# A fused normalise and quantised two-layer block: more work to GpSimd, identity built on the chip, a new pixel pairing, new orders

## The chip, the cores and the metric

The kernel runs on one core of one Trainium2 chip. The time is that of one launch on the device, in microseconds. Before the change: 70.01 us, median of 3 runs (69.95 to 71.6).

## The reference, cut to what matters

`x` is 8 images of 24 channels of 64 x 64 pixels. For each pixel, with all sums over its 24 channels:

```python
def conv_ref(x):                       # a gate per pixel
    m = sobel_complexity(x)            # edges of the mean over channels, scaled to 0..1
    steps = adaptive_steps(m)          # step widths from m
    V = v0 + v1 + v2 + v3              # how many of four walks visit the pixel
    return x * (V / (V + 1e-06))[:, None]

def ffn_ref(x, W1, b1, W2, b2):        # 24 -> 96 -> 24
    h = relu(qlinear(x, W1, b1))       # qlinear: products of fp8 (e5m2) values,
    return qlinear(h, W2, b2)          # result and result + bias rounded to fp16

def _gn(v, G=32, eps=1e-05): ...       # (g - m) / sqrt(s + eps)
def _ln_c(v, eps=1e-06): ...           # mean and variance over the channels
...
```

In the kernel this becomes: the input is centred and divided by its deviation over the channels (`inv_std`); that, times the gate's share, is the first branch, which is added to the input; the sum is normalised again (`norm2`), rounded to fp8, sent through the two quantised layers, and the result is added. When the normalised image is even, up to rounding, its edges are all zero and the visits are known beforehand (`flat_share`). The kernel computes that case, tests it at the end (`flag`), and repeats the work with computed visits only if the test says so. In the runs here it doesn't.

## The kernel before, in words

**Layout.** 128 partitions hold 256 pixels each of 24 channels, cut in 8 groups (`NG`) of 32 pixels (`GPIX`). A group's tile is 128 x 24 x 32, 768 numbers a partition. Statistics are made in four units of 1, 1, 2 and 4 groups (`UNIT_SIZE`).

**Stages of a group.** The sum over the channels (group 0: a VectorE reduction; groups 1 to 3: TensorE passes with the identity, `sum_channels`; groups 4 to 7 together: 24 passes in four parts, `sum_late_channels`). `centre` subtracts the mean (VectorE), `square` squares (ScalarE), `sum_squares` adds over channels on TensorE, then `take_var`, a square root on ScalarE (`first_std`), a reciprocal (`inverse_std`), the gain and a second variance (`conv_gain`), a second root and reciprocal, and `second_norm`. Then two branches:

- `conv` multiplies the centred tile by the gain into `result`, on GpSimd for groups 0, 1, 4, 5, 6 and on VectorE for 2, 3, 7. GpSimd then issues a DMA that adds the pixels to `result` (`add_pixels`).
- `quantise` makes fp8 values, two bytes of which form one bf16 word. Four TensorE transposes (`turn`) bring 96 rows = 24 channels x 4 to the partitions. ScalarE copies them (`copy_turned`). `first_layer` makes three hidden tiles of 128 rows and 1024 columns, each rounded to fp16 by ScalarE (`round_hidden`), biased and clipped by VectorE (`bias_relu`), and turned to fp8 (`quantise_hidden`). `second_layer` is 24 matmuls, ScalarE rounds (`round_ffn`), VectorE adds the second bias (`second_bias`) into `ffn_out`. For groups 0 to 5 GpSimd issues a second accumulating DMA (`add_ffn_by_dma`); for 6 and 7 VectorE adds (`add_ffn`), group 7 in halves.

**What sets the order.** Each engine has one order written out by hand (`first_groups` in each block); instructions start in that order as their semaphores allow. SP's queue issues the eight loads of pixels, then the stores of groups 0 to 6, each behind its second accumulate. ScalarE's queue issues the constants in two transfers at the start and the store of group 7 at the end. GpSimd's order has, besides the waits for its operands, five others:

```python
pool.wait_ge(s.scaled_var, 2)      # before conv(s, 0)
pool.wait_ge(s.norm2, 2)           # before conv(s, 1)
pool.wait_ge(s.ffn_out, 1)         # before conv(s, 4)
pool.wait_ge(s.hidden_act, 8)      # before conv(s, 5)
pool.wait_ge(s.hidden_act, 11)     # before conv(s, 6)
```

`keep_busy` issues three matmuls on a tile of zeros. `cast_weights` turns weights and biases to fp8 on VectorE after the centring of group 0. `unevenness` and `flag` are the test.

## Time and profile before

| | us |
|---|---|
| median of 3 runs | 70.01 |
| lowest, highest | 69.95, 71.6 |
| span of the profiled execution | 69.4 |
| busy: TensorE, VectorE, ScalarE, GpSimd | 53.4, 54.9, 44.2, 24.1 |

The profiled execution's own time is not given apart from its span; the span runs from the first to the last instruction. The mean granted TensorE clock over it is 0.948 of full speed. The page also counts 1372 instructions and 12.51 MB moved by DMA. Busy time of an engine counts its work, not its waiting; DMA-issuing instructions are counted apart, with the time until their data landed.

### The profile page before, as it was taken

The numbers are of one execution on the slowest core, as the hardware profiler recorded it, in microseconds if no ns is written. First come the engines' busy times: TensorE is split into PE (matmuls) and PEld (weight loads), VectorE is DVE, ScalarE is ACT, GpSimd is POOL, SyncE is SP. The second block draws the span as 40 slices with busy tenths as digits, with TensorE's granted clock in tenths as the row PEclk, the third lists the DMA queues.
The fourth block names the chain that finished last, engine by engine and source line by source line (L and its number), as shares of the span: only waits on it lengthen the run. The fifth ranks groups of instructions, "written<-read, shape, count | busy, mean of one in ns | idle before, by whom it ended". The sixth has DMA issues, their size and how long they took to land.

```text
span 69.4 us, 1372 instructions
## 1 busy us (share of the span) xinstructions
PE 53.4 (77%) x486; PEld 37.7 (54%) x486; DVE 54.9 (79%) x120; ACT 44.2 (64%) x60; POOL 24.1 (35%) x25
## 2 busy tenths in 40 slices
PE   2993999999999999948859969899898989700000
PEld 1323999999999999817126427355532644600000
DVE  2059934989799999999999999999999999981000
...
GB/s 0 291 403 404 413 402 232 9 0 0 0 184 71 198 0 0 130 101 57 170 9 73 216 218 282 209 189 200 302 218 202 296 214 331 240 241 125 395 177 11
DMA packets 4619, 12.51 MB, mean 180 GB/s; under 512 B 512, under 2 KB 640, under 8 KB 4608
## 3 DMA queue, kind: packets, MB, share of 16 engines
q0 software_dynamic: 2016, 5.51, 39.6%
q1 hardware_dynamic: 2160, 5.90, 22.2%
...
HBM read 3.72 MB, written 3.15 MB: 99 GB/s over the span
## 4 chain that ended last, share of the span: by engine, by line
PE 28%; DVE 23%; issue 15%; ACT 15%; DMA 7%; SPq 1%; DVEq 0%; ACTq 0%
ACT hidden_rounded L426 10%; PE ps_ffn L546 8%; DMA pixels<-in_x 7%; PE ps_ffn L534 6%; PE ps_ffn L564 4%; PE ps_hidden L564 4%; DVE hidden_q L852 3%; PE ps_ffn L619 3%; DVE hidden_act L843 3%; DVE result L812 3%; ACT packed_t L417 2%; DVE packed L831 2%; ACT ffn_rounded L436 2%; DVE inv_std L788 2%; DVE inv_std L817 2%
## 5 line engine op out<-in xcount | busy, mean ns | idle before, releaser
L426 ACT ACTIVATE hidden_rounded<-ps_hidden 128x1024 f16<-128x1024 f32 x24 | 23.9, 1049 | 0.5 <-PE ps_hidden L597 0.5
L343 POOL TENSOR_TENSOR result<-centred,gain 128x768 f32<-128x768 f32 x5 | 9.4, 1887 | 17.3 <-DVE scaled_var L805 14.7
L597 PE MATMUL ps_hidden<-packed_t,w1q 96*128 96x512 fp8e5 x48 | 13.9, 380 | 1.7 <-ACT packed_t L417 1.2
L331 POOL DMA_DIRECT2D result<-pixels x8 | 9.1, 1131 | 9.1 <-DVE result L812 7.9
L843 DVE TENSOR_SCALAR hidden_act<-hidden_rounded,b1q 128x1024 f16<-128x1024 f16 x24 | 11.6, 487 | 0.1
L395 ACT ACTIVATE squares<-centred 128x768 f32<-128x768 f32 (+1 forms) x9 | 6.7, 764 | 5.2 <-DVE centred L774 5.2
L619 PEld LDWEIGHTS ps_ffn<-w2q,hidden_q 128*128 128x128 fp8e5 x168 | 7.5, 98 | 3.7 <-DVE hidden_q L852 2.0
L619 PE MATMUL ps_ffn<-w2q,hidden_q 128*128 128x96 fp8e5 x168 | 8.3, 206 | 1.3 <-DVE square_sums L781 1.2
L337 POOL DMA_DIRECT2D result<-ffn_out x6 | 6.5, 1082 | 7.6 <-DVE ffn_out L860 7.6
L564 PEld LDWEIGHTS ps_ffn<-squares,fixed 128*128 128x128 f32 x72 | 8.7, 191 | 0.6
L564 PE MATMUL ps_ffn<-squares,fixed 128*128 128x128 f32 x72 | 8.9, 276 | 0.0
L852 DVE TENSOR_SCALAR hidden_q<-hidden_act 128x2048 uint16<-128x2048 uint16 (+1 forms) x16 | 8.8, 551 | 0.1
L436 ACT ACTIVATE ffn_rounded<-ps_ffn 128x768 f16<-128x768 f32 x7 | 7.5, 1068 | 0.5 <-PE ps_ffn L619 0.4
L774 DVE SCALAR_TENSOR_TENSOR centred<-ps_values,pixels 128x768 f32<-128x768 f32 (+1 forms) x9 | 7.5, 856 | 0.1
L831 DVE TENSOR_TENSOR packed<-centred,ps_values 128x768 fp8e5<-128x768 f32 x8 | 7.4, 945 | 0.0
L417 ACT ACTIVATE packed_t<-ps_turned 96x512 bf16<-96x512 bf16 x8 | 4.9, 613 | 3.4 <-PE ps_turned L582 3.4
L597 PEld LDWEIGHTS ps_hidden<-packed_t,w1q 96*128 96x128 fp8e5 x48 | 3.6, 97 | 5.5 <-ACT hidden_rounded L426 2.0
L632 PE MATMUL ps_ffn<-warm 128*128 128x512 bf16 x18 | 4.9, 382 | 1.4 <-ACT ffn_rounded L436 1.4
L546 PE MATMUL ps_ffn<-pixels,fixed 128*128 128x128 f32 x48 | 5.7, 276 | 0.0
L546 PEld LDWEIGHTS ps_ffn<-pixels,fixed 128*128 128x128 f32 x48 | 5.5, 192 | 0.0
L534 PE MATMUL ps_ffn<-pixels,fixed 128*128 128x128 f32 x36 | 4.4, 277 | 1.1 <-DMA pixels<-in_x 1.1
L534 PEld LDWEIGHTS ps_ffn<-pixels,fixed 128*128 128x128 f32 x36 | 4.2, 192 | 1.6 <-issue 1.6
...
## 6 DMA issues: line engine op xcount, KB each, us to landing
pixels<-in_x SPq DMA_DIRECT2D x8, 384.0 KB, 6.5
result<-pixels POOLq DMA_DIRECT2D x8, 384.0 KB, 4.6
out<-result SPq DMA_DIRECT2D x7, 384.0 KB, 4.3
result<-ffn_out POOLq DMA_DIRECT2D x6, 384.0 KB, 5.4
...
out<-result ACTq DMA_DIRECT2D x1, 384.0 KB, 3.2
...
```

The costliest lines, as they stand in the source:

```text
L331: pool.dma_start(result[:, n], pixels[:, n], accum_op=ALU.add).then_inc(s.residual[n], 16)
L343: nc.gpsimd.tensor_tensor(result[:, n], centred[:, n], group_values(gain, n), ALU.mult).then_inc(s.conv_pool, 1)
L426: nc.scalar.activation(hidden_rounded[:, i % HIDDEN_BUFS], ps_hidden[:, i % 2], ACT.Copy).then_inc(s.hidden_rounded, 1)
L436: nc.scalar.activation(ffn_rounded[:, n % 2].rearrange("p (h j) m b -> p h b (j m)", h=2)[:, lo:hi], ffn_banks(n)[:, lo:hi, 0:JP * CQ].rea ...
L534: last = nc.tensor.matmul(ps_channel[u][:, n - UNIT_START[u]], ident, pixels[:, n, c:c + CB, :], start=(c == 0), stop=(c == C - CB))
L546: last = nc.tensor.matmul(ps_late_channels, ident, pixels[:, 4:NG, c, :], start=(c == 0), stop=(c == C - 1))
L564: last = nc.tensor.matmul(ps_square[u][:, n - UNIT_START[u]], ident, squares[:, n, c * GPIX:(c + CB) * GPIX], start=(c == 0), stop=(c == C ...
L597: last = nc.tensor.matmul(ps_hidden[:, i % 2, b * BANK:(b + 1) * BANK], w1q[:, t * P:(t + 1) * P], packed_t[:, n % 2].bitcast(E5M2)[:, b:: ...
L619: last = nc.tensor.matmul(ffn_banks(n)[:, half, at * CQ:(at + 1) * CQ], hidden_q[:, n % 2, t, col * P:(col + 1) * P].bitcast(E5M2)[:, 0::2 ...
L831: nc.vector.tensor_tensor(packed[:, n % 2].rearrange("p j (c q) b -> p j c (q b)", q=Q), centred[:, n].rearrange("p c (j k) -> p j c k", j ...
L843: nc.vector.tensor_scalar(hidden_act[:, n % 2, t], hidden_rounded[:, (n * TILES + t) % HIDDEN_BUFS], b1q[:, t:t + 1], 0.0, ALU.add, ALU.ma ...
L852: nc.vector.tensor_scalar(hidden_q[:, n % 2, lo:hi], hidden_act[:, n % 2, lo:hi].bitcast(U16), 1.0 / 256, None, ALU.mult).then_inc(s.hidde ...
```

## The change

1. The channel sums of groups 4 to 7 come from GpSimd: `fold_channels` adds the two halves of the channels, then halves again, for two groups at a time, and VectorE copies the sums. The TensorE passes (`sum_late_channels`) are dropped.
2. The identity (fp32 and bf16) is made on GpSimd by two selects over a tile of ones; it is no longer loaded or cast. The constants are one transfer on SP's queue, between the loads of pixels 3 and 4. GpSimd does the casts of weights and biases.
3. All eight products (`conv`) are GpSimd's, and the five other waits are dropped. The accumulate of the sums of group 0 stands behind product 6, that of group 1 behind product 7.
4. The rows of the hidden layer are ordered so that tiles 0 and 1 have the same bias per row: one `bias_relu` covers both, and `quantise_hidden` covers all three tiles (group 7: two and one). The rounded hidden tiles have room for two groups.
5. The two pixels that share a bf16 word are sixteen apart in their group, not neighbours; the 96 rows are ordered q, c. The second layer's columns then come out in plain order, so `round_ffn` is a plain copy, and `copy_turned` copies fp32 words. The host arranges pixels and weights to fit.
6. The fast pass of the test multiplies the channel sums by `inv_std` and compares with `PEAK_LIMIT`; `flag` stands last on VectorE.
7. The stores of groups 6 and 7 are both ScalarE's. The orders of all engines are new; those of VectorE and ScalarE are only named here: quantisers of later groups, folded sums and biases stand in other places, and `square(1)` follows the first roots.

```diff
-SUM_SETS = [(0, 1), (1, 2), (2, 4), (4, 8)]
+SUM_SETS = [(0, 1), (1, 2), (2, 4), (4, 6), (6, 8)]
+FOLDED = range(4, NG)
...
-FIXED = {"ident": P, "share": PIX, "w1": Q * HIDDEN, "w2": TILES * CQ, "b1": TILES, "b2": 2 * CQ}
+TWIN = 64
+FIXED = {"share": PIX, "w1": Q * HIDDEN, "w2": TILES * CQ, "b1": 2, "b2": CQ}
...
-CONV_ON_POOL = [0, 1, 4, 5, 6]
-CONV_ON_VECTOR = [n for n in range(NG) if n not in CONV_ON_POOL]
+PEAK_LIMIT = C * FLAT * 2.0 ** 22
 ADD_BY_DMA = range(0, 6)
...
+        def hidden_acts(n, t):
+            return 2 * n + (1 if t < 2 else 2)
...
-            for n in range(NG - 1):
+                if n == 3:
+                    sp.dma_start(fixed[:], fixed_in).then_inc(weights_in, 16)
+            for n in range(6):
                 store(flat_pass, n)
             uneven_map = is_uneven(sp)
...
+            def make_identity():
+                link(nc.gpsimd.memset(ones[:], 1.0))
+                for tile in (ident, ident_bf):
+                    nc.gpsimd.affine_select(tile[:], ones[:], [[-1, P]], ALU.is_equal, 0.0, base=0,
+                                            channel_multiplier=1).then_inc(ident_ready, 1)
+            def cast_first():
+                pool.wait_ge(weights_in, 16)
+                nc.gpsimd.tensor_copy(w1q[:], w1_in, saturate=False).then_inc(first_weights, 1)
+                link(nc.gpsimd.tensor_copy(b1e[:], b1_in, saturate=False))
+                nc.gpsimd.tensor_copy(b1q[:], b1e[:]).then_inc(first_bias, 1)
+            def cast_second():
...
+            def fold_channels(n):
+                pair = (n - FOLDED.start) // 2
+                half = folded[:, pair]
+                pool.wait_ge(pixels_in[n], 16)
+                pool.wait_ge(pixels_in[n + 1], 16)
+                link(nc.gpsimd.tensor_tensor(half, pixels[:, n:n + 2, 0:12, :], pixels[:, n:n + 2, 12:24, :], ALU.add))
+                link(nc.gpsimd.tensor_tensor(half[:, :, 0:6, :], half[:, :, 0:6, :], half[:, :, 6:12, :], ALU.add))
+                link(nc.gpsimd.tensor_tensor(half[:, :, 0:3, :], half[:, :, 0:3, :], half[:, :, 3:6, :], ALU.add))
+                link(nc.gpsimd.tensor_tensor(half[:, :, 0, :], half[:, :, 0, :], half[:, :, 1, :], ALU.add))
+                nc.gpsimd.tensor_tensor(groups_pixels(folded_sums, range(2 * pair, 2 * pair + 2)).rearrange("p (g s) -> p g s", g=2),
+                                        half[:, :, 0, :], half[:, :, 2, :], ALU.add).then_inc(folded_ready, 1)
...
             def add_pixels(s, n):
-                if n in CONV_ON_POOL:
-                    pool.wait_ge(s.conv_pool, CONV_ON_POOL.index(n) + 1)
-                else:
-                    pool.wait_ge(s.conv_vector, CONV_ON_VECTOR.index(n) + 1)
+                pool.wait_ge(s.conv, n + 1)
...
             def first_groups(s):
-                pool.wait_ge(s.scaled_var, 2)
+                cast_first()
+                fold_channels(4)
+                fold_channels(6)
+                cast_second()
                 conv(s, 0)
                 add_pixels(s, 0)
-                pool.wait_ge(s.norm2, 2)
                 conv(s, 1)
                 add_pixels(s, 1)
+                conv(s, 2)
                 add_pixels(s, 2)
+                conv(s, 3)
                 add_pixels(s, 3)
-                pool.wait_ge(s.ffn_out, 1)
                 conv(s, 4)
-                add_ffn_by_dma(s, 0)
                 add_pixels(s, 4)
-                pool.wait_ge(s.hidden_act, 8)
                 conv(s, 5)
                 add_pixels(s, 5)
+                conv(s, 6)
+                add_ffn_by_dma(s, 0)
+                add_pixels(s, 6)
+                conv(s, 7)
                 add_ffn_by_dma(s, 1)
-                pool.wait_ge(s.hidden_act, 11)
-                conv(s, 6)
-                add_pixels(s, 6)
+                add_pixels(s, 7)
                 add_ffn_by_dma(s, 2)
-                add_pixels(s, 7)
                 add_ffn_by_dma(s, 3)
                 add_ffn_by_dma(s, 4)
                 add_ffn_by_dma(s, 5)
             nc.gpsimd.memset(eps_c[:], EPS_LN_C).then_inc(eps_ready, 1)
             nc.gpsimd.memset(eps_t[:], EPS_LN_T).then_inc(eps_ready, 1)
+            make_identity()
...
-                nc.scalar.activation(packed_t[:, n % 2], turned_group(), ACT.Copy).then_inc(s.turned_copied, 1)
+                nc.scalar.activation(packed_t[:, n % 2].bitcast(F32), turned_words(), ACT.Copy).then_inc(s.turned_copied, 1)
...
-                i = n * TILES + t
-                act.wait_ge(s.first_layer, i + 1)
-                if i >= HIDDEN_BUFS:
-                    act.wait_ge(s.hidden_act, i - HIDDEN_BUFS + 1)
-                nc.scalar.activation(hidden_rounded[:, i % HIDDEN_BUFS], ps_hidden[:, i % 2],
+                act.wait_ge(s.first_layer, n * TILES + t + 1)
+                if n >= 2:
+                    act.wait_ge(s.hidden_act, hidden_acts(n - 2, t))
+                nc.scalar.activation(hidden_rounded[:, n % 2, t], ps_hidden[:, (n * TILES + t) % 2],
                                      ACT.Copy).then_inc(s.hidden_rounded, 1)
...
-                nc.scalar.activation(ffn_rounded[:, n % 2].rearrange("p (h j) m b -> p h b (j m)", h=2)[:, lo:hi],
-                                     ffn_banks(n)[:, lo:hi, 0:JP * CQ].rearrange("p h (b m) -> p h b m", b=2),
-                                     ACT.Copy).then_inc(s.ffn_rounded, 1)
+                nc.scalar.activation(ffn_rounded[:, n % 2].rearrange("p (h i) m -> p h (i m)", h=2)[:, lo:hi],
+                                     ffn_banks(n)[:, lo:hi, 0:JP * CQ], ACT.Copy).then_inc(s.ffn_rounded, 1)
...
-            act.dma_start(fixed[:, 0:FIXED_AT["share"]], fixed_in[:, 0:FIXED_AT["share"]]).then_inc(ident_in, 16)
-            act.dma_start(fixed[:, FIXED_AT["share"]:], fixed_in[:, FIXED_AT["share"]:]).then_inc(weights_in, 16)
...
-            wait_result(act, flat_pass, NG - 1)
-            act.dma_start(out[NG - 1], result[:, NG - 1]).then_inc(flat_pass.stored, 16)
+            for n in (6, 7):
+                wait_result(act, flat_pass, n)
+                act.dma_start(out[n], result[:, n]).then_inc(flat_pass.stored, 16)
...
-            def sum_late_channels(part):
-                if part == 0:
-                    for n in range(4, NG):
-                        pe.wait_ge(pixels_in[n], 16)
-                    pe.wait_ge(sums_taken, 1)
-                for c in range(part * 6, (part + 1) * 6):
-                    last = nc.tensor.matmul(ps_late_channels, ident, pixels[:, 4:NG, c, :],
-                                            start=(c == 0), stop=(c == C - 1))
-                if part == 3:
-                    last.then_inc(sums_ready, 1)
...
             def first_groups(s):
                 sum_channels(1)
+                sum_squares(0)
                 sum_channels(2)
-                sum_squares(0)
                 sum_channels(3)
                 sum_squares(1)
-                sum_late_channels(0)
-                sum_late_channels(1)
-                sum_late_channels(2)
-                pe.wait_ge(ident_cast, 1)
+                pe.wait_ge(ident_ready, 2)
                 turn(s, 0)
-                sum_late_channels(3)
                 pe.wait_ge(first_weights, 1)
                 pe.wait_ge(var_taken, 1)
                 first_layer(s, 0, 0)
...
+                if lo in FOLDED:
+                    dve.wait_ge(folded_ready, i - 2)
+                    nc.vector.tensor_copy(sums, groups_pixels(folded_sums, range(lo - FOLDED.start, hi - FOLDED.start))).then_inc(sums_taken, 1)
...
-                nc.vector.tensor_tensor(packed[:, n % 2].rearrange("p j (c q) b -> p j c (q b)", q=Q),
-                                        centred[:, n].rearrange("p c (j k) -> p j c k", j=JP),
-                                        group_values(norm2, n).rearrange("p c (j k) -> p j c k", j=JP),
+                nc.vector.tensor_tensor(packed[:, n % 2].rearrange("p j (q c b) -> p (j q) c b", q=Q, b=2),
+                                        centred[:, n].rearrange("p c (b i) -> p i c b", b=2),
+                                        group_values(norm2, n).rearrange("p c (b i) -> p i c b", b=2),
...
-            def bias_relu(s, n, t):
+            def bias_relu(s, n, lo, hi):
                 dve.wait_ge(first_bias, 1)
-                dve.wait_ge(s.hidden_rounded, n * TILES + t + 1)
+                dve.wait_ge(s.hidden_rounded, n * TILES + hi)
                 if n >= 2:
-                    dve.wait_ge(s.hidden_q, 2 * (n - 1))
-                nc.vector.tensor_scalar(hidden_act[:, n % 2, t], hidden_rounded[:, (n * TILES + t) % HIDDEN_BUFS],
-                                        b1q[:, t:t + 1], 0.0, ALU.add, ALU.max).then_inc(s.hidden_act, 1)
+                    dve.wait_ge(s.hidden_q, n - 1)
+                nc.vector.tensor_scalar(hidden_act[:, n % 2, lo:hi], hidden_rounded[:, n % 2, lo:hi],
+                                        b1q[:, lo // 2:lo // 2 + 1], 0.0, ALU.add, ALU.max).then_inc(s.hidden_act, 1)
...
-                nc.vector.tensor_tensor(ffn_out[:, n].rearrange("p c (j k) -> p j c k", j=JP)[:, lo:hi],
-                                        ffn_rounded[:, n % 2, lo:hi].rearrange("p j (c q) b -> p j c (q b)", q=Q),
-                                        b2q[:, None, :].broadcast_to([P, hi - lo, 2 * CQ]).rearrange("p j (c k) -> p j c k", k=K),
+                nc.vector.tensor_tensor(ffn_out[:, n].rearrange("p c (i q) -> p i c q", q=Q)[:, lo:hi],
+                                        ffn_rounded[:, n % 2, lo:hi].rearrange("p i (c q) -> p i c q", q=Q),
+                                        b2q[:, None, :].broadcast_to([P, hi - lo, CQ]).rearrange("p i (c q) -> p i c q", q=Q),
...
-            def unevenness():
-                xall = xg[:].rearrange("p h s -> p (h s)")
+            def scaled_sums():
                 dve.wait_ge(inv_std_ready, UNITS)
-                link(nc.vector.tensor_scalar(channel_mean[:], channel_sums, 1.0 / C, None, ALU.mult))
-                link(nc.vector.scalar_tensor_tensor(rest[:], channel_mean[:], -float(C), channel_sums, ALU.mult, ALU.add))
-                link(nc.vector.tensor_tensor(xall, rest[:], inv_std[:], ALU.mult))
-                nc.vector.tensor_reduce(quad[:, 0:1], xall, AX_X, ALU.max,
+                nc.vector.tensor_tensor(xg[:].rearrange("p h s -> p (h s)"), channel_sums, inv_std[:], ALU.mult).then_inc(scaled_sums_ready, 1)
+            def partition_peaks():
+                dve.wait_ge(scaled_sums_ready, 1)
+                nc.vector.tensor_reduce(quad[:, 0:1], xg[:].rearrange("p h s -> p (h s)"), AX_X, ALU.max,
                                         apply_absolute_value=True).then_inc(peak_ready, 1)
...
```

## Rows read from the trace of the kernel before

**Rows 1.** Stretches of 6 us: busy of each engine, granted clock, DMA share, GB/s.

```profile
42.00:48.00 6.00, 5.63 (x69) 3.52 (x67) 6.00 (x12) 6.00 (x9) 4.04 (x4) 1.00 1.01 211
48.00:54.00 6.00, 5.19 (x50) 2.34 (x48) 5.90 (x15) 6.00 (x9) 2.64 (x3) 1.00 1.00 236
```

**Rows 2.** Chain of waits in order of time: start, us, what.

```profile
13.26 4.02 PE ps_ffn L546 x36
...
17.50 1.39 PE ps_ffn L546 x12
...
62.24 0.56 DVE result L871
```

**Rows 3.** What SyncE's transfer queue waited for: us in total, times, longest.

```profile
SPq L308 <- DMA result<-ffn_out: 57.2, 6, 35.2
SPq L317 <- DMA out<-result: 3.3, 1, 3.3
```

**Rows 4.** Timeline of VectorE: start, us, instruction.

```profile
39.72 0.57 DVE L843 TENSOR_SCALAR hidden_act<-hidden_rounded,b1q 128x1024 f16<-128x1024 f16 x1
...
56.49 0.55 DVE L860 TENSOR_TENSOR ffn_out<-ffn_rounded,b2q 128x768 f16<-128x768 f16 x1
...
59.98 0.96 DVE L871 TENSOR_TENSOR result<-result,ffn_out 128x768 f32<-128x768 f32 x1
```

**Rows 5.** Timeline of GpSimd, products and accumulate issues.

```profile
15.57 1.82 POOL L343 TENSOR_TENSOR result<-centred,gain 128x768 f32<-128x768 f32 x1 [14.70 <-DVE scaled_var L805]
17.70 1.01 POOL L331 DMA_DIRECT2D result<-pixels  x1 [0.32 <-DVE centred L774]
18.45 2.12 POOL L343 TENSOR_TENSOR result<-centred,gain 128x768 f32<-128x768 f32 x1
...
38.16 1.85 POOL L343 TENSOR_TENSOR result<-centred,gain 128x768 f32<-128x768 f32 x1
40.30 1.19 POOL L331 DMA_DIRECT2D result<-pixels  x1 [0.30 <-POOL result L343]
...
57.58 1.06 POOL L337 DMA_DIRECT2D result<-ffn_out  x1 [1.62 <-DVE ffn_out L860]
```

**Rows 6.** Issue of the last accumulate (57.58 us); last number: us until landed.

```profile
result<-ffn_out POOLq DMA_DIRECT2D x1, 384.0 KB, 5.9
```

**Rows 7.** Stretches of 1 us, columns as in group 1.

```profile
11.00:12.00 1.00, 1.00 (x12) 1.00 (x11) 0.40 (x2) 0.26 (x1) 0.00 (x0) 1.00 0.42 160
62.00:63.00 1.00, 0.00 (x0) 0.00 (x0) 0.69 (x2) 0.00 (x0) 0.00 (x0) 0.61 0.14 35
63.00:64.00 1.00, 0.00 (x0) 0.00 (x0) 0.00 (x0) 0.00 (x0) 0.00 (x0) 0.50 0.35 134
```

**Rows 8.** Page, part 3: DMA queues with packets, MB, share of 16 engines.

```profile
q0 software_dynamic: 2016, 5.51, 39.6%
q1 hardware_dynamic: 2160, 5.90, 22.2%
```

**Rows 9.** Groups by line and shape: busy us, mean ns of one, idle before.

```profile
L843 DVE TENSOR_SCALAR hidden_act<-hidden_rounded,b1q 128x1024 f16<-128x1024 f16 x24 | 11.6, 487 | 0.1
...
L436 ACT ACTIVATE ffn_rounded<-ps_ffn 128x768 f16<-128x768 f32 x7 | 7.5, 1068 | 0.5 <-PE ps_ffn L619 0.4
L831 DVE TENSOR_TENSOR packed<-centred,ps_values 128x768 fp8e5<-128x768 f32 x8 | 7.4, 945 | 0.0
...
L395 ACT ACTIVATE squares<-centred 128x768 f32<-128x768 f32 x7 | 5.7, 836 | 1.9 <-DVE centred L774 1.9
...
L852 DVE TENSOR_SCALAR hidden_q<-hidden_act 128x2048 uint16<-128x2048 uint16 x8 | 5.5, 688 | 0.0
...
L417 ACT ACTIVATE packed_t<-ps_turned 96x512 bf16<-96x512 bf16 x8 | 4.9, 613 | 3.4 <-PE ps_turned L582 3.4
...
L754 DVE TENSOR_REDUCE ps_values<-pixels 128x32 f32<-128x768 f32 x1 | 1.5, 1455 | 0.0
...
L744 DVE CAST w1q<-fixed 96x384 fp8e5<-96x384 f32 x1 | 0.4, 356 | 0.0
```

327 lines of the change are left out of this document (153 added, 174 removed).

## The prediction

> **What bounds the kernel now.** I read the busy time by stretch first. From 42 to 54 us VectorE is busy 11.90 of 12 us and ScalarE all 12 [rows 1]: two engines fill that stage together, and the DMA engines' share is 1.01 and 1.00, so a third resource is full as well. The chain of waits shows what sets the start: TensorE's four parts of late channel sums (4.02 and 1.39 us, split by one transpose) stand on it [rows 2], and its last computed piece is the addition of group 7, over at 62.80. But the span is 69.4. What fills the rest is in the transfer queue's waits: SyncE waited 57.2 us in all for accumulating DMAs, and 3.3 us at the end for its last store [rows 3]. The sums of group 5 are ready at 57.04 [rows 4], their accumulate is issued at 57.58 [rows 5] and takes 5.9 us to land [rows 6], so at 63.5; only then can store 5 go, and store 6, whose data were added by 60.94 [rows 4], stands behind it on SP. Meanwhile the DMA engines do next to nothing from 62 to 64 (0.14 and 0.35) [rows 7].
>
> So there are two chains: compute, and GpSimd's issues with the DMA engines behind them. The queues say how heavy the second is [rows 8]: 39.6% of 69.4 us over 14 accumulates (8 of pixels, 6 of sums) is 1.96 us each with all 16 engines; 22.2% over 15 plain transfers is 1.03 each. Accumulates and stores together: 14 x 1.96 + 8 x 1.03 = 35.7 us.
>
> **What the change takes off the compute chain.** *TensorE:* 48 passes of late sums, 5.4 us [rows 2], go. *VectorE:* three products of the quantiser's size and form, 3 x 0.945 = 2.8; six casts of weights and one of the identity, the largest 0.356 [rows 9], about 1.7 together (bound 2.5). Twin tiles: 16 bias instructions of 1024 become 8 of 2048; the quantiser of the same kind takes 0.688 for 2048 and the bias 0.487 for 1024 [rows 9], so I take 0.75 for a twin, 8 x (0.974 - 0.75) = 1.8 (bounds 0 and 2.3). Merged quantisers: seven times two fixed parts become one, about 1.0. Two steps of the evenness test leave, a third of a quantiser's elements each, 0.8 (bounds 0.6 and 1.9). Together 8.1 us of 54.9 (the casts and part of the products lay beside other work). *ScalarE:* the copy of the transposes takes 256 words instead of 512 halves. 0.613 at 512 and 0.836 at 768 give 0.87 ns an element, so 0.39, 8 x 0.22 = 1.8. The rounding of the second layer no longer interleaves: 1.068 at 768 becomes 0.836, as the squares of the same size [rows 9]; 7 x 0.23 = 1.6. If word size or stride cost nothing, both are 0; bounds 0 and 3.4, and I take 3.4.
> The input: 3.57 MB instead of 3.72, and pixels 1 no longer share with the constants. At the before's 0.40 MB/us, over in the twelfth microsecond (share 0.42) [rows 7], pixels 1 land near 4.3, the constants at 7.3, pixels 5 at 9.3 (2.79 MB), pixels 7 at 11.2: on SP's queue the constants stand ahead of pixels 4 to 7 and hold them for 1.1. Centring groups 4 to 7 waits for the folds, not for these. The first layer's weights come with the constants and then GpSimd's cast, near 8.3; the first layer wants them after 12. The identity must be there by then: two selects after 0.9, bound 0.1 to 1.9 each (nothing, a product of six times the elements), covered by the 11 warm-up matmuls.
> Walking the new orders with these durations, the first transpose is copied near 12.7 instead of 17.5, the sums of group 5 are out near 52 instead of 57.0, and the last addition ends near 57.5: compute is some 5 us earlier.
>
> **One price against that.** The quantiser now reads `centred` in steps of 64 and 128 bytes, before in runs of 32 bytes. The one VectorE row that reads SBUF in 128-byte steps is the channel sum of group 0: 1.455 us for 768 elements, against 0.945 for the quantiser [rows 9]. Bounds per quantiser 0 and +0.51, for eight 0 and +4.1; I take +2 by halves, since that row is a reduction during the input, and both ends go into the range. It delays the additions, not GpSimd's chain, and costs 0 to 0.7 at the end. The sums of the second layer write runs of 8 bytes instead of 16; no row has such a step, 0 to +0.3 per instruction (half its 0.55), and the same cover.
> The Trainium skill ("SBUF — State Buffer", Door 1: The DMA port swizzle) says that lines are 16 bytes and that a stride with one access per line pays a penalty; by that rule every quantiser pays. The trace agrees as far as that one row goes.
>
> **The other chain.** GpSimd now casts, folds, forms all products and issues the same 14 accumulates. One product is 1.82 to 1.85 us (the one at 18.45 counts 2.12, but the issue in front of it ran until 18.71) [rows 5]. A fold of a pair of groups is 768, 384, 192, 64 and 64 elements; in proportion to the product 1.85 x 1568 / 768 = 3.8; no row shows a small GpSimd operation, and I take 0.1 on the whole for what each costs besides. Four self-waits lie in it: 0, or the 0.30 between product and issue [rows 5]; I take 0.1 each. Two folds: 8.6 (bounds 7.6 and 10.2). The second casts: no row for GpSimd, between VectorE's 0.8 and twice that; 1.2. Product 0 starts at 9.3 + 8.6 + 1.2 = 19.1, where it started at 15.57. Product to product with one issue is 2.88 early (15.57 to 18.45); in the busy stage 2.14 go by before the issue and the issue takes 1.19 instead of 1.01, 3.3 at most [rows 5]; at 2.9, product 6 starts at 36.5. Now the queue position matters: the accumulate of sums 0 stands behind product 6, at 38.4 (before 36.3), with pixels 6 behind it; that of sums 1 stands behind product 7, near 42.3.
> The DMA engines: pixels 0 to 5 are through by about 39. Left are two pixel and six sum accumulates and eight stores, 8 x 1.96 + 8 x 1.03 = 23.9. From 39.8 (issue plus 1.4) that is 63.7 if the engines never rest. They rested 1.5 us of two in the before while the last accumulate landed [rows 7]; store 5 waits for that again, +1.5. GpSimd's products now run with no wait that places them, so some start against VectorE's bias and quantiser instructions: I allow 1.2 (below). From the last byte to the end 2.3 us as now (about 67.1 to 69.4). Sum 63.7 + 1.5 + 1.2 + 2.3 = **68.7 us of span**. The before's span of 69.4 stands 0.6 under its median of 70.01, so I forecast 69.3. Moving store 6 to ScalarE's queue takes it from behind store 5, inside the 1.5. The test of evenness moves last on VectorE, near 58: at no cost, since the stores cover it by some 8 us; with that cover gone, under 1.
>
> **Rivals.**
> *A, the backlog swallows the gain* (my forecast): 68.6 to 71.4, chance 0.36. For it: the full DMA share from 42 us.
> *B, it comes through in part.* GpSimd is never held (-1.2), its folds are at the low bound (-0.8), stores 0 to 4 fill the hole (-1.0): 66.3 to 68.6, near 67. If the whole compute gain reached the end, 52 + (69.4 - 57.04) - 1.4 (store 6) + 0.6 is 63.6, which the 23.9 us of transfers forbid unless they start earlier. For it: VectorE and ScalarE both gain. Chance 0.35.
> *C, GpSimd and VectorE shut each other out, slower.* The before starts its products behind counts (scaled_var 2, norm2 2, ffn_out 1, hidden_act 8 and 11), and they fall on quantisers. Where one product's end met a bias (39.72, product over at 40.01), that took 0.57 instead of 0.487 [rows 4, 9], and was over 0.28 after the product's end [rows 5]: as if its stream had waited for the whole rest. The change drops these waits. A bias or quantiser that meets a fresh product is then held up to 1.85 - 0.2 = 1.65. With four such meetings VectorE loses 6.6, more than its 5 of gain, ffn_out 0 is late, and GpSimd, in order, holds pixels 6 and product 7 behind it. Everything from 39.8 on moves 3 to 4: 73. It decides from 2 us of delay of the first sum accumulate (40.5). Against it: no row shows a meeting longer than 0.3 us. Chance 0.29.
> The Trainium skill ("SBUF — State Buffer", Who interferes with whom) says that VectorE's two-port modes and GpSimd hold a shared port pair for a whole instruction, and the other is fully blocked. By that rule C is the outcome, 73; this trace agrees on 0.3 us of overlap only.
> *D, the new forms save ScalarE nothing* (word copy, plain rounding): additions 1.7 later, still under the transfers, 69.5; inside A.
>
> **Numbers.** 69.3. The range 66.4 to 73.3 holds B without its lowest tenth and C without its dearest part. Within 2% (68.6 to 71.4, about what a measurement of this kernel can tell from no change) 0.36, faster 0.35, slower 0.29.
>
> **What would show it.** Right: late passes gone from TensorE; the first product near 19; GpSimd without idle time until about 44; DMA share near 1 from 40 to the last accumulate; ffn_out 5 near 52 and the last addition near 57.5 with the end near 68.7. Wrong: bias instructions over 1 us beside products (C); quantisers at 0.95 or 1.45 settle the stride; the first store before 42 and idle DMA engines after 50 would mean B. If GpSimd's small folds cost over 0.5 each, the sum is 1.5 too low.

## The result and the profile after

The changed kernel takes 82.53 us, median of 4 runs (82.02 to 83.76); the kernel before, run on the same chip, 70.81 (69.95 to 71.61). The ratio is 1.175, 95% interval 1.165 to 1.185: slower by some 12 us, outside the range that was given (66.4 to 73.3), on the side of rival C. The ratio is taken over the executions within 1.5% of the fastest of each kernel, so it differs a little from the quotient of the two medians. The profiled execution has a span of 80.6 us.

**Busy time** of the changed kernel, from part 1 of its page:

```profile
PE 54.7 (68%) x438; PEld 36.3 (45%) x438; DVE 65.9 (82%) x94; ACT 41.9 (52%) x60; POOL 38.7 (48%) x47
```

VectorE should have lost 8.1 us and regained 2 for the new pairing (4.1 at most). It went up instead, from 54.9 to 65.9. Groups by line and shape of the changed kernel (busy us, mean ns of one, idle before) say where:

```profile
L843 DVE TENSOR_TENSOR packed<-centred,ps_values 128x768 fp8e5<-128x768 f32 x8 | 11.6, 1446 | 0.1
L864 DVE TENSOR_SCALAR hidden_q<-hidden_act 128x3072 uint16<-128x3072 uint16 x7 | 9.3, 1344 | 0.0
L855 DVE TENSOR_SCALAR hidden_act<-hidden_rounded,b1q 128x2048 f16<-128x2048 f16 x8 | 7.6, 945 | 0.2 <-issue 0.2
L855 DVE TENSOR_SCALAR hidden_act<-hidden_rounded,b1q 128x1024 f16<-128x1024 f16 x8 | 7.2, 905 | 0.6 <-ACT hidden_rounded L479 0.3 <-issue 0.3
...
L823 DVE SCALAR_TENSOR_TENSOR scaled_var<-gain,scaled_once 128x128 f32<-128x128 f32 x1 | 1.8, 1782 | 0.0
```

The quantiser is at 1446, not 945: the upper bound of the stride, to 0.01 us. The single bias went from 487 to 905 ns although nothing about it changed [rows 9]. That is no property of the instruction. The timeline of VectorE in the changed kernel (start, us, instruction), which answers to [rows 4], shows it spread over a few cases:

```profile
16.50 1.74 DVE L820 SCALAR_TENSOR_TENSOR scaled_once<-gain,square_sums 128x32 f32<-128x32 f32 x1
...
24.86 2.35 DVE L855 TENSOR_SCALAR hidden_act<-hidden_rounded,b1q 128x2048 f16<-128x2048 f16 x1
...
31.18 1.79 DVE L855 TENSOR_SCALAR hidden_act<-hidden_rounded,b1q 128x1024 f16<-128x1024 f16 x1
...
39.10 3.90 DVE L855 TENSOR_SCALAR hidden_act<-hidden_rounded,b1q 128x2048 f16<-128x2048 f16 x3
...
53.94 3.71 DVE L864 TENSOR_SCALAR hidden_q<-hidden_act 128x3072 uint16<-128x3072 uint16 x1
...
72.85 1.02 DVE L883 TENSOR_TENSOR result<-result,ffn_out 128x384 f32<-128x384 f32 x2
```

Beside it the timeline of GpSimd of the same kernel, which answers to [rows 5]:

```profile
16.38 1.81 POOL L373 TENSOR_TENSOR folded<-pixels 128x768 f32<-128x768 f32 x1
...
21.65 1.82 POOL L395 TENSOR_TENSOR result<-centred,gain 128x768 f32<-128x768 f32 x1
...
24.58 2.07 POOL L395 TENSOR_TENSOR result<-centred,gain 128x768 f32<-128x768 f32 x1
...
30.58 2.10 POOL L395 TENSOR_TENSOR result<-centred,gain 128x768 f32<-128x768 f32 x1
...
39.98 2.06 POOL L395 TENSOR_TENSOR result<-centred,gain 128x768 f32<-128x768 f32 x1
...
53.22 0.88 POOL L389 DMA_DIRECT2D result<-ffn_out  x1 [8.17 <-DVE ffn_out L872]
...
54.37 2.45 POOL L395 TENSOR_TENSOR result<-centred,gain 128x768 f32<-128x768 f32 x1
...
69.06 1.02 POOL L389 DMA_DIRECT2D result<-ffn_out  x1 [0.95 <-DVE ffn_out L872]
```

Read the two together. The twin bias of 24.86 starts 0.28 after a product that runs until 26.65, and ends at 27.21, 0.56 behind it. The bias of 31.18 starts inside the product of 30.58 (over at 32.68) and ends at 32.97. `scaled_once`, a step of 0.19 us elsewhere, starts 0.12 after the first fold addition of the second pair and takes 1.74. Where one step meets one product, it ends its own length, less some 0.2 at most, after GpSimd's instruction. There are eight such places; five are in the fences, the other three are `norm2` at 28.57 (1.20) and 43.89 (1.32) and `scaled_var` at 37.40 (1.78). With the lengths that each step has when alone, the lost time is 1.55 + 1.60 + 0.98 + 1.31 + 1.49 + 2.10 + 1.02 + 2.76 = 12.8 us, 1.55 of it from a fold, the rest from products. With the forecast's savings and the stride's upper bound that makes 54.9 - 8.1 + 4.0 + 12.8 = 63.6 against 65.9 seen. Most of the remaining 2.3 is in how steps are counted. Neighbouring steps of VectorE overlap a little in the trace: before, the durations of its 120 steps add up to 61.6 us for 54.9 of busy time, and in the changed kernel those of 94 steps to 70.6 for 65.9. The overlap shrinks by 1.9 us, so that the steps that go take less off the busy time than their durations say.

The stretches of the changed kernel fit this. Stretches of 6 us of the changed kernel (columns as in [rows 1]):

```profile
30.00:36.00 6.00, 2.73 (x18) 1.67 (x17) 6.00 (x6) 1.91 (x5) 3.55 (x3) 0.81 0.72 131
...
42.00:48.00 6.00, 1.28 (x7) 0.58 (x6) 5.93 (x7) 2.01 (x4) 2.75 (x3) 0.67 0.49 89
48.00:54.00 6.00, 6.00 (x37) 3.40 (x35) 6.00 (x10) 3.35 (x4) 0.78 (x2) 0.50 0.01 3
...
66.00:72.00 6.00, 5.32 (x81) 3.56 (x78) 4.61 (x9) 3.91 (x6) 1.88 (x2) 1.00 1.07 312
```

Where [rows 1] had a DMA share of 1.01 and 1.00, there is now 0.49 and 0.01, and TensorE works 1.28 us of six: VectorE alone is full. The waits of the changed kernel (us in total, times, longest) name the two that starve:

```profile
POOL result L389 <- DVE ffn_out L872: 15.4, 5, 8.2
PE ps_turned L616 <- DVE packed L843: 7.5, 3, 4.2
```

TensorE waited 4.2 us for a quantiser until 46.73, and after such pauses its granted clock stood at 0.50, the lower of its two levels (48 to 54). The SyncE queue waited longer for the accumulates than in [rows 3]:

```profile
SPq L320 <- DMA result<-ffn_out: 66.6, 6, 50.7
```

The last addition is over at 73.87 (62.80 before), the span 6.7 later (6.6 before). The tail is unchanged; compute is 11 us later.

### The profile page after: what moved, and what is told of

Read it like the earlier page. It is cut to its first block, busy times and chain, and to the rows that moved or that the text cites. A ratio compares the mean times of both kernels' runs of the same rounds, so it can differ in the third digit from the quotient of the medians.

```text
span 80.6 us, 1256 instructions
## 1 busy us (share of the span) xinstructions
PE 54.7 (68%) x438; PEld 36.3 (45%) x438; DVE 65.9 (82%) x94; ACT 41.9 (52%) x60; POOL 38.7 (48%) x47
## 3 DMA queue, kind: packets, MB, share of 16 engines
q1 hardware_dynamic: 2160, 5.97, 20.0%
## 4 chain that ended last, share of the span: by engine, by line
DVE 41%; PE 32%; ACT 10%; issue 8%; ACTq 0%; DVEq 0%
DVE hidden_act L855 10%; PE ps_ffn L651 8%; PE ps_hidden L631 7%; DVE packed L843 7%; DVE centred L792 7%; PE ps_ffn L749 6%; PE ps_ffn L664 5%; ACT hidden_rounded L479 5%; DVE ps_values L834 4%; ACT ffn_rounded L489 3%; DVE scaled_once L820 3%; DVE inv_std L829 2%; PE ps_turned L616 2%; PE ps_ffn L584 2%; ACT packed_t L471 2%
## 5 line engine op out<-in xcount | busy, mean ns | idle before, releaser
L395 POOL TENSOR_TENSOR result<-centred,gain 128x768 f32<-128x768 f32 x8 | 16.4, 2053 | 3.3 <-DVE gain L818 3.3
L855 DVE TENSOR_SCALAR hidden_act<-hidden_rounded,b1q 128x2048 f16<-128x2048 f16 (+1 forms) x16 | 14.4, 925 | 0.9 <-issue 0.5
L389 POOL DMA_DIRECT2D result<-ffn_out x6 | 6.4, 1072 | 15.4 <-DVE ffn_out L872 15.4
L598 PE MATMUL ps_ffn<-squares,ident 128*128 128x128 f32 x72 | 9.2, 280 | 3.8 <-ACT squares L449 3.8
L843 DVE TENSOR_TENSOR packed<-centred,ps_values 128x768 fp8e5<-128x768 f32 x8 | 11.6, 1446 | 0.1
L598 PEld LDWEIGHTS ps_ffn<-squares,ident 128*128 128x128 f32 x72 | 8.4, 191 | 5.4 <-issue 5.4
L864 DVE TENSOR_SCALAR hidden_q<-hidden_act 128x3072 uint16<-128x3072 uint16 (+2 forms) x9 | 10.4, 1172 | 0.0
L616 PE MATMUL ps_turned<-ident_bf,packed 128*96 128x128 bf16 x32 | 4.0, 259 | 7.5 <-DVE packed L843 7.5
L616 PEld LDWEIGHTS ps_turned<-ident_bf,packed 128*96 128x96 bf16 x32 | 3.0, 147 | 9.9 <-DVE packed L843 9.3
L664 PE MATMUL ps_ffn<-warm 128*128 128x512 bf16 x18 | 5.6, 423 | 0.6 <-ACT ffn_rounded L489 0.5
L749 PE MATMUL ps_ffn<-warm 128*128 128x512 bf16 x11 | 4.9, 632 | 1.3 <-DVE warm L1143 1.3
L872 DVE TENSOR_TENSOR ffn_out<-ffn_rounded,b2q 128x768 f16<-128x768 f16 (+1 forms) x9 | 4.4, 508 | 0.7 <-ACT ffn_rounded L489 0.7
```

Source lines behind the costliest of these rows:

```text
L395: nc.gpsimd.tensor_tensor(result[:, n], centred[:, n], group_values(gain, n), ALU.mult).then_inc(s.conv, 1)
L598: last = nc.tensor.matmul(ps_square[u][:, n - UNIT_START[u]], ident[:], squares[:, n, c * GPIX:(c + CB) * GPIX], start=(c == 0), stop=(c = ...
L616: last = nc.tensor.transpose(turned_group()[:, j * P:(j + 1) * P], packed[:, n % 2, j].bitcast(BF16), ident_bf[:])
L664: nc.tensor.matmul(ps_ffn[:, i % 2] if n < NG - 1 else ps_turned[:], warm[:, 0:P], warm[:], start=True, stop=True)
L749: nc.tensor.matmul(ps_ffn[:, i % 2], warm[:, 0:P], warm[:], start=True, stop=True)
L843: nc.vector.tensor_tensor(packed[:, n % 2].rearrange("p j (q c b) -> p (j q) c b", q=Q, b=2), centred[:, n].rearrange("p c (b i) -> p i c ...
```

## The experiments

Each is the changed kernel or the kernel before with the edit that is shown. The kernel before ran beside each, at 70.8 to 71.3 us in the median; where intervals are given they are of the ratio to it.

**Meetings by themselves.** A kernel of its own starts one product of the real size and then one VectorE step, 0.3 us later.

```python
nc.vector.tensor_copy(scr[:, 0:32], vals[:, 0:32]).then_inc(go, 1)   # the product starts
link(nc.vector.tensor_reduce(scr[:, 32:64], ..., AX_X, ALU.add))     # PSUM alone, 0.42 us
link(f())                                                            # the step to be met
```

> This kernel computes nothing of the reference; it measures single VectorE instructions of the case, first alone, then each issued about 0.5 us after GpSimd has begun a product of 128x768. Theory (GpSimd and VectorE shut each other out): the bias of 2048, the merged quantiser of 3072 and the two-input step of 128 end only after the product, so they take up to 1.5 us more than alone (bias 0.75, quantiser 0.95, two-input step 0.29), whatever their own size; the fp8 quantisers, which read one operand from PSUM, and the reciprocal take the same as alone. Three merged quantisers issued just before a product delay it or are delayed by it once. Rival (both only slow each other down in proportion): the two-input step of 0.29 gains under 0.2, the bias under 0.4. Stride: the quantiser that reads steps of 64 and 128 bytes takes 1.45, the one with runs of 32 bytes 0.95; the one that reads runs of 64 bytes and writes in steps of 48 bytes tells whether writing costs the same (1.45) or nothing (0.95).

VectorE's timeline in that kernel, then GpSimd's:

```profile
12.57 1.54 DVE L70 TENSOR_SCALAR ha<-hr,b 128x2048 f16<-128x2048 f16 x2 [4.27 <-DMA px<-in_x]
...
29.68 2.06 DVE L70 TENSOR_SCALAR ha<-hr,b 128x2048 f16<-128x2048 f16 x1
...
35.27 1.66 DVE L72 SCALAR_TENSOR_TENSOR s<-s 128x128 f32<-128x128 f32 x1
...
37.54 0.95 DVE L75 TENSOR_TENSOR pkn<-px,vals 128x768 fp8e5<-128x768 f32 x1
...
43.87 0.95 DVE L71 TENSOR_SCALAR hq<-ha 128x3072 uint16<-128x3072 uint16 x1
```

```profile
29.39 1.80 POOL L53 TENSOR_TENSOR prod<-px,gain 128x768 f32<-128x768 f32 x1 [28.95 <-DVE scr L90]
...
44.04 2.44 POOL L53 TENSOR_TENSOR prod<-px,gain 128x768 f32<-128x768 f32 x1 [0.61 <-DVE scr L100]
```

The bias of two tiles takes 0.77 alone (two in 1.54) and 2.06 when met; the small step 0.31 alone and 1.66 met; the quantiser 0.95 both times. Started first, the quantisation of hidden values keeps its 0.95, and the product behind it needs 2.44 for 1.80; of three in a row the first goes, the product follows, and the other two wait: 4.42 us in all instead of some 2.9. So each engine shuts the other out for the rest of its instruction, for some forms and not for others. The strided read costs 1.45 against 0.95, alone too.

**The kernel before without its five placing waits.** Only `pool.wait_ge(...)` lines are taken out:

```diff
-                pool.wait_ge(s.scaled_var, 2)
-                pool.wait_ge(s.norm2, 2)
-                pool.wait_ge(s.ffn_out, 1)
-                pool.wait_ge(s.hidden_act, 8)
-                pool.wait_ge(s.hidden_act, 11)
```

> The kernel before with the five waits dropped that place products 0, 1, 4, 5 and 6, and nothing else. Lock theory: three or four products start against two-input steps and biases, each holds VectorE up to 1.65 us, VectorE loses about 5 to 8 us and ends that much later: 74 to 77 us. Rival (the backlog of transfers decides): products and their accumulates start earlier, nothing else changes: 69 to 70.5 us.

It took 79.76 us, ratio 1.130 (1.119 to 1.142): 9 us, more than the 74 to 77 that I expected. All five products met a step (at 13.33, 17.38, 38.09, 41.99 and 50.05), 9.0 us in all. VectorE's row and GpSimd's of one of them:

```profile
41.99 2.80 DVE L838 TENSOR_SCALAR hidden_act<-hidden_rounded,b1q 128x1024 f16<-128x1024 f16 x1
```

```profile
42.04 2.46 POOL L343 TENSOR_TENSOR result<-centred,gain 128x768 f32<-128x768 f32 x1
```

The bias stands 0.05 us *ahead* of the product by the trace and is held all the same, and the product takes 2.46 instead of 1.8. An accumulate issue of GpSimd is still open there (41.48 to 42.67), but an issue need not hold anything: in the kernel without product work below, a merged quantisation that starts inside one (44.70, the issue from 44.56 to 45.78) takes its usual 0.96, so I put the held time down to the product. Three quarters of the whole loss are had without any other part of the change.

**The change with its pixels paired as neighbours again.** The second layer's rounding interleaves again with it, as before the change; nothing else is touched. The quantiser's lines, the changed kernel's with a minus:

```diff
-packed[:, n % 2].rearrange("p j (q c b) -> p (j q) c b", q=Q, b=2), centred[:, n].rearrange("p c (b i) -> p i c b", b=2)
+packed[:, n % 2].rearrange("p j (c q) b -> p j c (q b)", q=Q), centred[:, n].rearrange("p c (j k) -> p j c k", j=JP)
```

> The changed kernel with the pixel pairing of before (neighbours share a word, rounding of the second layer interleaves again); all else as changed. If VectorE bounds the changed kernel: eight quantisers save 0.50 each, 4.0 us, less up to 1.7 for the dearer rounding on ScalarE: 78 to 80 us against 82.5. If the transfers bound it, the stride was hidden: 82 to 83.

It took 81.54 us, ratio 1.158 (1.148 to 1.167). The quantiser was back at 946 ns and 4.0 us of work gone, but only 1.0 of them reached the end, where I expected 78 to 80 us: single biases now averaged 1156 ns against 905, as the steps slid to other products.

**Products 2, 3 and 7 back on VectorE**, in the changed kernel, with no placing waits:

```diff
+CONV_ON_POOL = [0, 1, 4, 5, 6]
-                    conv(s, n)
+                    if n in CONV_ON_POOL:
+                        conv(s, n)
+                conv(s, 2)      # VectorE, behind quantise(s, 2); 3 and 7 alike
```

> The changed kernel with products 2, 3 and 7 on VectorE again, behind the quantisers of the same groups; GpSimd's placing waits stay dropped. Lock theory: VectorE works 2.8 us more but is held by three products fewer, each worth up to 1.65 to 3: 79 to 82.5. Rival (GpSimd's backlog decides): GpSimd is free 6 us earlier, 78 to 80. If neither: VectorE's 2.8 is added, 85.

84.77 us, ratio 1.191 (1.175 to 1.207), where I expected 79 to 82.5: a miss, and an instructive one. VectorE's row shows three biases in a row (1.83 us of work) held by two products in a row:

```profile
39.66 6.58 DVE L866 TENSOR_SCALAR hidden_act<-hidden_rounded,b1q 128x2048 f16<-128x2048 f16 x3
```

How many products GpSimd forms is not what counts; where each falls is.

**The change without the work of the products.** Each product is cut to one channel, the rest of the tile is loaded while the transfers idle:

```diff
-nc.gpsimd.tensor_tensor(result[:, n], centred[:, n], group_values(gain, n), ALU.mult)
+nc.gpsimd.tensor_tensor(result[:, n, 0:1], centred[:, n, 0:1], group_values(gain, n)[:, 0:1], ALU.mult)
+                sp.dma_start(result[:, n], x[n]).then_inc(filled[n], 16)
```

> The changed kernel, but each GpSimd product works on 1 channel of 24, and the rest of its tile is filled by eight extra loads of x while the transfers idle (12 to 20 us); the product of 23 channels is left out. Theory (VectorE steps are held by products): of some 13 us of held time about 1.5 to 2 belong to the folds, so 11 go; the last addition comes at 63 to 66 instead of 73.9 and the time is 71 to 75 us. Rival (the new orders, the folds or TensorE's half clock cost the time): 79 us or more, with the bias steps at 0.75 and the span hardly shorter.

72.22 us (72.02 to 72.28): 10.3 less than the changed kernel. All orders, the stride, the folds, the input order and the filler matmuls are still there. VectorE's busy time is 54.9 (11.0 less), the single bias is at 485 ns, and TensorE and its clock are back by themselves:

```profile
42.00:48.00 6.00, 5.17 (x64) 3.25 (x63) 5.20 (x9) 4.44 (x7) 3.04 (x5) 1.00 0.46 97
```

One meeting is left, that of `scaled_once` with a fold (1.73 at 15.88). The 10.3 us hold GpSimd's own time for the products too, but GpSimd had time to spare (15.4 us of waiting for sums above). The half clock was a consequence: no fill was added here, and TensorE's mean granted clock went from 0.858 to 0.941.

**The change with its late channel sums back on TensorE** and no folds:

```diff
-                fold_channels(4)
-                fold_channels(6)
+                sum_late_channels(0)       # TensorE; parts 1 and 2 follow,
+                sum_late_channels(3)       # part 3 behind turn(s, 0)
```

> The changed kernel with the late channel sums back on TensorE as before and no folds. Theory: the folds hold only 1 or 2 small steps (about 1.5 us) and their removal lets the products start 8 us earlier, onto other steps that they can hold, and TensorE gets 5.4 us back: 80 to 84 us, no clear gain. Rival (the folds' 8.6 us on GpSimd and the late additions behind them are the cost): 77 us or less.

84.97 us (83.84 to 86.0): no gain, as expected, though 1 us above the range. Product 0 now starts at 10.66, 11 us earlier, and with it the meetings (`scaled_var` of 32 values 0.99 in the mean, `norm2` 0.86).

**The useful parts on the kernel before.** Twin tiles with one bias, merged quantisation of hidden values, the shorter test of evenness, store 6 on ScalarE; all placing waits stay.

```diff
-                bias_relu(s, n, 0)
-                bias_relu(s, n, 1)
+                bias_relu(s, n, 0, 2)
-                quantise_hidden(s, n, 0, 2)
-                quantise_hidden(s, n, 2, 3)
+                quantise_hidden(s, n, 0, 3)
```

> The kernel before with only twin tiles and one bias for two, the merged quantisation of hidden, the shorter evenness test with its flag last, and store 6 on ScalarE; its quantisers, sums, division of products and all placing waits stay. Theory: VectorE loses 1.8 (bias) + 1.0 (merged) + 0.8 (evenness) of 54.9 us and nothing is held: 67 to 69 us. Rival: the larger steps come later than the two halves did and TensorE waits for them: 70 to 71.5.

71.20 us of 12 runs, ratio 1.010 (1.006 to 1.014): no gain, where I expected 67 to 69; the rival's range holds it. VectorE's busy time fell by 1.5 only (3.6 expected), and ScalarE, full in [rows 1] too, is still at 6.00 of 6 from 42 to 54. The row of 48 to 54 in this kernel:

```profile
48.00:54.00 6.00, 4.96 (x43) 2.44 (x43) 5.47 (x10) 6.00 (x8) 3.25 (x3) 1.00 1.01 232
```

**The change with its products placed.** Products 2, 3 and 7 on VectorE, five waits, pairs of steps set side by side behind them, and the accumulate of pixels 5 moved behind product 6:

```diff
+                pool.wait_ge(s.scaled_var, 2)    # fold 6: beside centrings 4, 5
+                pool.wait_ge(s.scaled_var, 3)    # product 0: beside centrings 6, 7
+                pool.wait_ge(s.norm2, 3)         # product 1: beside quantisers 2, 3
+                pool.wait_ge(s.norm2, 4)         # product 4: beside quantisers 4, 5
+                pool.wait_ge(s.ffn_out, 1)       # products 5, 6: beside quantisers 6, 7
                 conv(s, 5)
-                add_pixels(s, 5)
                 conv(s, 6)
                 add_ffn_by_dma(s, 0)
+                add_pixels(s, 5)
...
                 centre(6)
-                bias_relu(s, 0, 0, 2)
                 centre(7)
+                bias_relu(s, 0, 0, 2)            # and so at quantisers 2/3, 4/5, 6/7
```

> The changed kernel with products 2, 3 and 7 on VectorE, the other five and the second fold on placing waits, and VectorE's order altered in five places so that quantisers or centrings stand in pairs behind those waits. Theory: held time falls from 13 to about 3 us while the three products add 2.9: 65.9 falls to 59 and the time is 73 to 76 us. Rival (orders, stride, folds and clock cost the time, not the meetings): 80 us or more, as with the three products moved alone (84.8).

77.67 us, ratio 1.098 (1.087 to 1.109): 7.1 less than with the same division, no waits and the changed kernel's order. VectorE's busy time is 58.7, as worked out, but the time is 1.7 above the range that I expected from it. The last two experiments tell why.

**Three terms alone**, all on the kernel without product work (72.22), so that no product of full size meets anything; the folds still can.

The neighbour pairing, with the edit shown above:

> As e5 (the changed kernel with 23 of 24 channels of each product left out), and pixels paired as neighbours again, so that the quantiser takes 0.95 instead of 1.45. In e5 VectorE was busy 54.9 of 70.6 us and idle some 4 us between its steps, so if VectorE bounds the kernel the 4.0 us come off in good part: 69 to 70.5 us against 72.2. If the stride lies beside waits for ScalarE and TensorE (as the idle rows from 58 us on suggest for the last groups) it is worth at most 1 us: 71.2 to 72.2.

70.35 us (12 runs), ratio to the kernel before 0.993 (0.987 to 0.999). The pairing is worth 1.9 us here, twice what it was among the meetings, but that isn't the stride alone. The first quantiser is over 0.5 earlier, `scaled_once` now comes before the second fold and takes 0.19 instead of 1.73, and the centring of group 4 starts 1.6 us earlier (16.38 for 18.01). The step without and with the neighbour pairing:

```profile
15.88 1.73 DVE L824 SCALAR_TENSOR_TENSOR scaled_once<-gain,square_sums 128x32 f32<-128x32 f32 x1
```

```profile
15.71 0.19 DVE L827 SCALAR_TENSOR_TENSOR scaled_once<-gain,square_sums 128x32 f32<-128x32 f32 x1
```

Against it, the interleaving rounding is dearer on ScalarE. How the 1.9 divide among these is not shown. And even with the products' work left out, this design only draws level with the kernel before.

The late sums on TensorE, with the edit shown for them:

> As e5, and the late channel sums on TensorE as before, without the folds. The folds' work leaves 5.4 us on TensorE if they are a gain, and one held small step (scaled_once 1.74 for 0.2): if the folds help, this is slower than e5 by 1 to 3 us, 73 to 75; if they only hold small steps and come late, it is 70.5 to 72.

75.09 us: in this order the folds help, by 2.9. A wait of 2.79 us appears on VectorE until 18.55, for the deviation of group 1. Its sums of squares were taken at 14.62, but ScalarE's root (18.21) stands behind the copy of the first transposes, and that copy waits 5.94 us, until 17.93, for a transpose behind three parts of the late passes. So the 2.9 are the passes together with this place in ScalarE's order.

The constants on ScalarE's queue:

```diff
-                if n == 3:
-                    sp.dma_start(fixed[:], fixed_in).then_inc(weights_in, 16)
+            act.dma_start(fixed[:], fixed_in).then_inc(weights_in, 16)
```

> As e5, and the constants loaded from ScalarE's queue ahead of everything, not between pixels 3 and 4. The casts then start 3 to 4 us earlier and pixels 4 to 7 land up to 1 us earlier, pixels 0 later. If the later input delays the whole chain: 71 to 71.7 us against 72.2; if VectorE's queue of steps hides it: 72 to 72.5.

74.32 us, 2.1 slower and outside both expectations. With the constants on a second queue pixels 0 come at 5.66 instead of 3.90, and the last addition is 2.2 later. The late first tile is 1.8 us. But the folds meet other steps too: `gain` takes 1.41 at 11.17 and `scaled_var` 0.87 at 12.84, while `scaled_once`, 1.73 in the kernel without this edit, is free. What the arrival alone costs at the end is not shown.

**Two tiles straight from PSUM**, on the kernel of the kept parts:

```diff
+DIRECT = [n * 3 + 2 for n in (6, 7)]
+nc.vector.tensor_scalar(hidden_act[:, n % 2, lo:hi], ps_hidden[...], b1q[...], 0.0, ALU.add, ALU.max)
```

> As e7 (the parts kept on the kernel before), with the copy of turned words, and VectorE takes the third tile of groups 6 and 7 straight from PSUM, without ScalarE's rounding to fp16 ahead of the bias: ScalarE, which was busy from 36 to 62 us without a gap in e7, loses 2 x 1.07 us, VectorE gains 2 x 0.6. If ScalarE bounds the second half: 69.5 to 70.3 us against 71.2. If VectorE and TensorE come right behind it: 70.5 to 71.3.

71.17 us, ratio 1.007 (1.001 to 1.012): nothing. ScalarE is not alone at the bound in the second half: in this kernel VectorE is busy 5.97 of 6 us from 48 to 54, and ScalarE's last but one rounding waits 3.56 us for TensorE. No version of the whole computation that I tried beats the kernel before.

**Which steps are held.** Eight forms, alone and behind a product:

```python
nc.vector.scalar_tensor_tensor(outc[:], g,  -1.0 / C, px[:, 2], ...)   # g: sums in PSUM
nc.vector.scalar_tensor_tensor(outc[:], gs, -1.0 / C, px[:, 2], ...)   # gs: sums in SBUF
```

> A kernel of its own: eight step forms of VectorE alone, then each started 0.3 us behind a GpSimd product. Theory (a step is held where it reads two operands from SBUF, or one in a fast 16-bit form, and runs free where one of two operands lies in PSUM): centring with PSUM sums 0.95 alone and met, with SBUF sums 0.95 alone and about 2.1 met; VectorE product 0.95 and 2.1; quantiser with SBUF scale 0.95 and 2.1; reduction of one SBUF tile 1.46 both; second bias in fp16 with two SBUF inputs 0.55 and 1.9; small step of two SBUF operands 0.2 and 1.5; small step with one operand in PSUM 0.3 both. Rival (type and form decide: fp32 steps of 768 elements go free, small or 16-bit ones are held): all 768-element fp32 forms 0.95 to 1.46 met as alone, and both small steps held.

Four rows of VectorE, each met by a product 0.3 us old: centring with its sums in PSUM, the same with them in SBUF, a step of 32 values with two operands in SBUF, a step of 128 with one in PSUM.

```profile
20.85 0.96 DVE L89 SCALAR_TENSOR_TENSOR outc<-vals,px 128x768 f32<-128x768 f32 x1
...
23.04 2.33 DVE L90 SCALAR_TENSOR_TENSOR outc<-gain,px 128x768 f32<-128x768 f32 x1
...
36.54 1.56 DVE L97 SCALAR_TENSOR_TENSOR s<-s 128x32 f32<-128x32 f32 x1
...
38.72 0.29 DVE L98 SCALAR_TENSOR_TENSOR s<-s,vals 128x128 f32<-128x128 f32 x1
```

Alone they take 0.96, 0.96, 0.19 and 0.29. The quantiser with its scale in SBUF is held as well (2.33 for 0.96), the second bias too (1.93 for 0.56); the reduction of one SBUF tile is not (1.47 for 1.44). So size and type do not decide (128 values with both operands in SBUF took 1.66 in the first small kernel, 128 with one in PSUM 0.29 here): a step with two operands in SBUF is held, the same step with one of them in PSUM runs free. To that come the 16-bit steps of one operand, bias and quantisation of hidden values (met in the first small kernel). By these rows this kernel's centrings and quantisers are a safe cover because `channel_sums` and `norm2` lie in PSUM.

**Placed, with neighbours paired** (both edits above):

> As e8 (five products and the second fold placed, three products on VectorE) with the neighbour pairing of the kernel before, so quantisers of 0.95 instead of 1.45. VectorE loses 4.0 us of work, but the pairs behind which the products hide shrink from 2.8 to 1.8 us: if the stride was worth its 1.9 and nothing new is held, 75.5 to 76.2; if the shorter cover brings meetings back or the transfers after 60 us set the end, 77 to 78.

76.43 us, ratio 1.088 (1.080 to 1.097). The last addition is over at 63.64, nearly as early as before (62.80), and yet the span is 74.7: 11.1 us behind it instead of 6.6. Two stretches of this kernel:

```profile
42.00:48.00 6.00, 4.69 (x52) 2.78 (x53) 6.00 (x7) 5.23 (x8) 5.69 (x4) 1.00 0.02 3
...
66.00:72.00 6.00, 0.00 (x0) 0.00 (x0) 0.00 (x0) 0.00 (x0) 0.00 (x0) 0.54 0.98 363
```

With the compute chain nearly repaired (one meeting is left, the merged quantisation at 44.87 with 2.57 us), the other chain of the forecast sets the end: the DMA engines rest while products 5 and 6 are formed in one row (42.31 to 46.63) with the accumulates behind them, that of pixels 5 too by the edit above, and then have a backlog until 72.

**Product 4 to VectorE, product 5 earlier:**

```diff
-CONV_ON_POOL = [0, 1, 4, 5, 6]
+CONV_ON_POOL = [0, 1, 5, 6]      # conv(4) on VectorE behind its gain; 5 behind norm2 4, 6 behind ffn_out 1
```

> As e14, but product 4 on VectorE (right behind the gain it needs), product 5 on GpSimd beside quantisers 4 and 5 and its accumulate issued at once, product 6 alone beside quantisers 6 and 7. Accumulates 4 to 6 are issued some 4, 8 and 2 us earlier. Theory (in e14 the transfers set the end, idle 6 us from 42 to 48 and full from 48 to 71): the span falls by 2 to 4 us, 72.5 to 74.5 us against 76.4, with the last addition where it was (63 to 64.5). Rival (compute sets the end): the added VectorE product costs its 0.95, or nothing changes, 76.4 to 77.5.

73.59 us, ratio 1.041 (1.030 to 1.053), while the last addition is 1 us *later* (64.60). The same stretch now moves data:

```profile
42.00:48.00 6.00, 4.99 (x61) 3.12 (x59) 5.40 (x9) 4.35 (x7) 3.80 (x4) 0.99 0.34 77
```

The last meeting is gone here too. So 8.9 of the 11.7 us are won back by placing work, dividing it anew and pairing neighbours again.

## Why the prediction was wrong, step by step

**The step that failed** is one sentence: "some start against VectorE's bias and quantiser instructions: I allow 1.2". Measured, that term is up to 10.3 us (82.53 against 72.22, which holds the products' own time too); VectorE's held time beside products is 11.3 of the 12.8 us above. Rival C named the mechanism and what marks it ("bias instructions over 1 us beside products"), but was wrong in two sizes. It counted four meetings; there were eight, one of them with a fold and four of them at small variance and scale steps, which I had not thought of as anything that could be held. And it priced each at 1.65 at most; one place cost 2.10 (the three biases of 39.10), another 2.76 (the quantisation of 53.94), and with two products in a row 4.8 (the products back on VectorE). C also said that GpSimd, in order, would hold product 7: the first accumulate of sums, forecast for 38.4, was issued at 53.22, and product 7 began at 54.37. Its own time of 73 was 9.5 short. The argument against it, "no row shows a meeting longer than 0.3 us", was the mistake of reasoning: the trace could not show one, since the five waits that the change drops are what kept the products off the steps. With them gone the kernel before shows 9.0 us of held time at once. The rows did hold the hint, the bias of 39.72 [rows 4], and the Trainium skill ("SBUF — State Buffer", Who interferes with whom) states full blocking for VectorE's two-port modes. The runs agree as far as the blocking goes, with the numbers above; which mode a step ran in no trace shows. By that rule the forecast should have been C, which names the right mechanism and still falls short of the time.

**The stride**: 0.50 for each quantiser, the upper bound; 4.0 us of VectorE's time, and at the end 1.0 us for the whole pairing among the meetings, 1.9 without products (a fold's meeting and the rounding included). I took 2 on VectorE and 0 to 0.7 at the end. The cover that I named, additions that end before the transfers do, was not there.

**The compute chain "some 5 us earlier"**: wrong without any meeting too. With products and stride away the last addition ends at 61.54, not at 57.5. The input was 2.7 us late (below), and the first transpose was copied from 13.63 there, not near 12.7. The walk added up engine times, but from 42 on that chain runs from engine to engine: in that kernel VectorE is busy 13.0 of the 18 us to 60 and TensorE 14.6. How the 4 us divide between the late input and the hand-overs I have not separated; that part stays open.

**The smaller terms.** What held: late passes gone from TensorE, and the folds worth it (2.9 us in this order). ScalarE's copy is 373 ns (0.39 forecast) and its plain rounding 811 (0.836). The twin bias alone is 0.75 and the merged quantisation saves 1.0, both as taken. The fold took 4.4 us for a pair with its waits against the 4.3 in the sum, partly by luck: the elements of its five additions are 1472, not the 1568 that I used, which make some 4.0. The constants landed at 10.0 instead of 7.3, and pixels 5 at 12.05 instead of 9.3: I had the stream 2.7 us early, and the first product, forecast for 19.1, began at 21.65. Moving stores and the test of evenness cost nothing visible: the tail is 6.7 against 6.6.

**The backlog (A)** was no cause in the changed kernel (DMA share 0.01 from 48 to 54, and 6.7 us behind the last addition as before). It is a true second bound that shows as soon as the first is lifted: between the last two kernels the time behind the last addition falls from 11.1 to 6.7 us, though that addition comes 1 us later.
